# Cross-attention pairs written out as straight code, the projection between two value tiles, three residual operations on three steps

## What is computed

```python
q = proj(layernorm(x), Wq, bq); k = proj(ctx, Wk, bk); v = proj(ctx, Wv, bv)   # 16 heads of 16
scores = where(mask, clip(q @ k.T / 4, -50, 50), -50)
ctx_out = softmax(scores) @ v
delta = clip(residual_scale, 0, 0.3) * (ctx_out @ Wo.T + bo)
x = x + layernorm(delta) * ln_gamma + ln_beta
```

## Time and profile before

| what | value |
|---|---|
| device time, median of three runs | 1797.5 us (1793.64 to 1798.63) |
| device time of the profiled execution | 1795.94 us |
| its span, first to last instruction | 1794.1 us |
| cross-attention loop, first scores to last step | 538 to 1661 us of the span |
| mean granted clock of TensorE | 0.946 of full speed |

### The profile page before, as it was taken

The page is one execution under the profiler, slowest core; times in us unless marked ns, Lnnn a source line. Parts: engine busy times, 40 slices in busy tenths (PEclk is TensorE's granted clock), DMA queues, the critical chain, the costliest instruction groups (busy, mean ns, idle before and its releaser), DMA issues. The chain is left out here.

```text
span 1794.1 us, 48379 instructions
## 1 busy us (share of the span) xinstructions
PE 1594.6 (89%) x18290; PEld 1341.1 (75%) x18290; DVE 1454.5 (81%) x2513; ACT 1117.9 (62%) x2155; POOL 734.8 (41%) x743
## 2 busy tenths in 40 slices
PE   5899999998739999999999999999999999999464
PEld 5888888886528878787887787877877878788233
DVE  3788877875467898888888988888889888898698
ACT  3566555664337776676676666766766667677463
POOL 1565555553163443443343434433434344343133
PEclk9999999998769999999999999999999999999678
DMA  6000000000221111111111111111111111110001
GB/s 183 1 1 2 2 1 1 1 0 1 85 79 47 48 48 39 45 47 48 36 47 48 47 42 42 47 48 37 47 48 48 46 38 47 48 47 2 1 11 31
DMA packets 41611, 66.85 MB, mean 37 GB/s; under 512 B 7749, under 2 KB 40194, under 8 KB 41282
## 3 DMA queue, kind: packets, MB, share of 16 engines
q1 hardware_dynamic: 41410, 63.93, 12.3%
HBM read 62.08 MB, written 1.84 MB: 36 GB/s over the span
## 5 line engine op out<-in xcount | busy, mean ns | idle before, releaser
L1146 POOL TENSOR_TENSOR xa_CW<-xa_CTX,xa_CH 128x500 fp32r<-128x500 f32 x187 | 283.1, 1514 | 676.6 <-ACT xa_CH L1337 674.3
L1365 DVE TENSOR_TENSOR xl_ACC<-xl_ACC,xl_PB 125x896 f32<-125x896 f32 x320 | 422.0, 1319 | 36.1
L1329 ACT ACTIVATE xl_PB<-banks,xl_BIB,xl_SCB 125x896 f32<-125x896 f32 x384 | 400.8, 1094 | 74.5 <-PE banks L1203 74.5
L1356 DVE TENSOR_SCALAR xl_PB<-xl_PB 125x896 f32<-125x896 f32 x384 | 269.9, 703 | 57.2 <-ACT xl_PB L1329 53.6
L1311 ACT ACTIVATE xl_V<-banks 125x256 f32<-125x256 f32 x384 | 147.5, 384 | 179.6 <-PE banks L1170 179.6
L1170 PE MATMUL banks<-xa_WVhigh,xa_CH 128*125 128x256 f32 x768 | 239.5, 312 | 0.0
L1170 PE MATMUL banks<-xa_WVlow,xa_CH 128*125 128x256 f32 x768 | 217.0, 283 | 0.0
L1170 PE MATMUL banks<-xa_WVhigh,xa_CW 128*125 128x256 f32 x768 | 216.1, 281 | 0.0
L1219 PE MATMUL banks<-xl_PB,xl_V 125*32 125x112 f32 x6144 | 199.8, 271 | 2.5 <-DVE xl_PB L1356 1.7
L1302 ACT ACTIVATE xl_KXhigh<-banks,xa_bk 128x500 fp32r<-128x500 f32 x192 | 130.3, 679 | 104.2 <-PE banks L1170 104.2
L1170 PE MATMUL banks<-xa_CH,xa_WKhigh 128*128 128x500 f32 x384 | 152.5, 397 | 33.8 <-POOL xl_ONES L1108 27.7
(11 more groups left out here) (235 smaller groups left out, 4074.5 us busy)
## 6 DMA issues: line engine op xcount, KB each, us to landing
xa_CTX<-in_ctxT SPq DMA_DIRECT2D x93, 500.0 KB, 3.6
fw_WO<-in_W_o SPq DMA_DIRECT2D x1, 2048.0 KB, 17.7
xq_WR<-in_w_gating SPq DMA_DIRECT2D x1, 2048.0 KB, 9.5
X<-in_x SPq DMA_DIRECT2D x1, 1792.0 KB, 10.1
out<-ff_R SPq DMA_DIRECT2D x16, 112.0 KB, 1.9
fw_QUT<-in_W_quT SPq DMA_DIRECT2D x1, 1536.0 KB, 12.3
xa_CTX<-in_ctxT SPq DMA_DIRECT2D x1, 1500.0 KB, 14.8
xq_WL<-in_w_linear SPq DMA_DIRECT2D x1, 1024.0 KB, 11.7
```

Source lines behind the costliest of these rows:

```text
L1146: nc.gpsimd.tensor_tensor(context_piece(CW, i), context_piece(CTX, i), context_piece(CH, i), ALU.subtract).then_inc(ctx_low, 1)
L1329: nc.scalar.activation(PB[t % PR][:, :, :], banks[0:TK, 2 * i:2 * i + KT, 0:QW], ACT.Exp, scale=SCB[j][:, t:t + 1], bias=BIB[j][:, t:t + 1 ...
L1356: nc.vector.tensor_scalar(pt, pt, E_HI, E_LO, ALU.min, ALU.max).then_inc(clipped, 1)
L1365: nc.vector.tensor_tensor(ACC[j][:, :, :], prev[:, :, :], PB[t % PR][:, :, :], ALU.add).then_inc(summed, 1)
```

## The change

It does four things, all within `cross_loop`. The loop over pairs 1 to 14 becomes fourteen written-out copies on every engine. `project` moves on TensorE from ahead of both value tiles to between the first and the second. The three operations of `add_delta` move on GpSimd from step 8 to the ends of steps 6, 8 and 9, and its last wait, on its own addition, goes. To feed them, part 3 of `NORM` moves from step 7 to 6, and `delta_rstd` on ScalarE from step 6 to 5.

```diff
-    PROJECT, NORM = 3, {4: (0, 1), 5: (2,), 7: (3,), 10: (4, 5), 11: (6,)}
+    PROJECT, NORM, ADD_DELTA = 3, {4: (0, 1), 5: (2,), 6: (3,), 10: (4, 5), 11: (6,)}, (6, 8, 9)
...
         def pairs(eng, body):
 
-            body(0, True, False)
-            with eng.Fori(1, PAIRS - 1) as g:
-                body(g, False, False)
-            body(PAIRS - 1, False, True)
+            for g in range(PAIRS):
+                body(g, g == 0, g == PAIRS - 1)
...
-                def add_delta(g):
-
-                    pool.wait_ge(dn_ready, g + 1)
-                    nc.gpsimd.tensor_tensor(DL[:, :], DL[:, :], GAM[:, :], ALU.mult).then_inc(affine, 1)
-                    pool.wait_ge(affine, g * 2 + 1)
-                    nc.gpsimd.tensor_tensor(DL[:, :], DL[:, :], BET[:, :], ALU.add).then_inc(affine, 1)
-                    pool.wait_ge(affine, g * 2 + 2)
-                    xg = X[:, bass.ds(g, 1), :]
-                    nc.gpsimd.tensor_tensor(xg, xg, DL[:, :].unsqueeze(1), ALU.add).then_inc(x_added, 1)
-                    pool.wait_ge(x_added, g + 1)
+                def add_delta(g, step):
+
+                    if step == 0:
+                        pool.wait_ge(dn_ready, g + 1)
+                        nc.gpsimd.tensor_tensor(DL[:, :], DL[:, :], GAM[:, :], ALU.mult).then_inc(affine, 1)
+                    elif step == 1:
+                        pool.wait_ge(affine, g * 2 + 1)
+                        nc.gpsimd.tensor_tensor(DL[:, :], DL[:, :], BET[:, :], ALU.add).then_inc(affine, 1)
+                    else:
+                        pool.wait_ge(affine, g * 2 + 2)
+                        xg = X[:, bass.ds(g, 1), :]
+                        nc.gpsimd.tensor_tensor(xg, xg, DL[:, :].unsqueeze(1), ALU.add).then_inc(x_added, 1)
...
-                        if s == 8 and not first:
-                            add_delta(g - 1)
+                        if s in ADD_DELTA and not first:
+                            add_delta(g - 1, ADD_DELTA.index(s))
...
-                add_delta(PAIRS - 1)
+                for step in range(len(ADD_DELTA)):
+                    add_delta(PAIRS - 1, step)
...
-                def values(n, u, early=False):
-
-                    for i in range(2):
+                def values(n, u, tiles, early=False):
+
+                    for i in tiles:
...
+                        if more(last, s, 1):
+                            values(n + 1, (u + 1) % STEPS, (0,))
                         if s == PROJECT and not first:
 
                             pe.wait_ge(k_ready, n + K_AHEAD)
                             project(g - 1)
                         if more(last, s, 1):
-                            values(n + 1, (u + 1) % STEPS)
+                            values(n + 1, (u + 1) % STEPS, (1,))
...
-                        if s == 6 and not first:
+                        if s == 5 and not first:
                             delta_rstd(g - 1)
```

More of the change, by code:

```diff
@@ L1281, in _ @@
                     if p == 1:
-                        values(0, 0, early=True)
+                        values(0, 0, (0, 1), early=True)
                 pairs(pe, pair)
```

## The result

The changed kernel takes 1722.49 us in the median of four runs (1722.20 to 1724.10), the kernel before 1796.58 us: a ratio of 0.9591 with an interval of 0.9574 to 0.9607. The profiled execution has a span of 1720.7 us, 73.4 less than before. The forecast was 1731, with a range from 1720 to 1752.

A forecast was written before the change was run, and what follows sets the result against it. TensorE was taken as the bound, the gain being the excess of five long steps per pair. 29.1 + 20.4 - 4.2 + 7.6 + 12.0 = 64.9 us off 1795.94 gave 1731 us, range 1720 to 1752.

The forecast's parts named there:

- The jump: Step 11, before each of 13 jumps back: goes from 7.67 to 5.43 us, 29.1 us won.
- the rival of streams running dry: Written-out pairs on TensorE: instruction fetch falls behind, 2.24 us a hole; with three a pair, 1825 us; chance 0.02.
- The clock: Step 0 after each of 13 jumps: without the gap TensorE's clock stays up, 7.33 to 5.76 us, 20.4 us won.
- The rival built on that rule: Step 0 of the pairs: TensorE's clock falls even without the gap, the 20.4 us stay, 1751 us; chance 0.05.
- What the gap had covered: Pair boundaries: late VectorE costs 0.35 us at each of 13, 0.31 won from pair 14 to 15; together -4.2 us.
- The projection: Step 3: goes from 7.08 to 6.55 us, the keys then waiting for VectorE's read of the projection; 7.6 us won.
- The residual operations: Steps 9 and 10: spreading GpSimd's three operations removes their excess of 0.86 us in 14 pairs, 12.0 us won.
- The rival in which VectorE becomes the second bound: Steps 0, 3, 9 and 10: VectorE stays as late as before, blocking by GpSimd only moves; 1749 us, chance 0.22.

The follow-up runs named there:

- 6: Changed kernel with the engine loop back on TensorE alone, the other engines written out; span 1744.7 us in one profiled execution.
- 7: Changed kernel with the engine loop back on every engine but TensorE; span 1729.0 us in one profiled execution.
- 9: Changed kernel with a loop of two pairs per round, so 6 jumps instead of 13; span 1750.4 us in one profiled execution.
- 1: Kernel before with its loop over pairs written out, nothing else changed; 1731.15 us, ratio 0.9662.
- 4: Changed kernel with the three residual operations back in step 8, the norm's part 3 in step 7 and `delta_rstd` in step 6; 1733.42 us, ratio 0.9667.
- 8: Kernel before with VectorE's loop alone written out, the other engines still looping; 1772.72 us, span 1770.9, in one profiled execution.
- 2: Changed kernel with the engine loop over pairs back on all engines; 1760.53 us, ratio 0.9828.
- 3: Changed kernel with the projection ahead of both value tiles again; 1725.41 us, ratio 0.9618.
- 10: Changed kernel with VectorE's read of the projection ahead of the addition of tile 0 in step 3; 1721.02 us, ratio 0.9599.

## Why the prediction was right, and where it was not

**The jump** (29.1 forecast, 29.3 measured): right, and shown. TensorE's own jump makes the gap (6), the other four lie inside it (7), it goes by the number of jumps (9). In straight code TensorE had no hole in any pair, so the rival of streams running dry fell. VectorE's straight code had at least one, of 0.35 us, in step 7 of pair 14 of experiments 1, 4 and 8.

**The clock** (20.4 and 20.3): the size was right, its rule not. I took "gap, then low clock" as one thing. With the gaps in place the clock fell behind 13, 8, 4 and 1 of 13 jumps in four kernels and behind 3 of 6 in a fifth. The gap's length alone does not decide: step 11 was 7.33 long ahead of one fall in experiment 2, and 7.96 with no fall behind it in experiment 9. Without a jump no pair of any kernel saw a fall. So removing the gap is sufficient, as forecast, but 20 us was the price of this one loop, which met the fall at every jump; why it did, and the others not, stays open. The page of the Trainium skill (TensorE: Matmul & The Clock Gate, section "Why this matters for your kernels") speaks of longer idle gaps than these; the clock fell after gaps of 2 us, so here the measurement decides. The rival built on that rule fell.

**What the gap had covered** (-4.2 forecast, +0.7 measured): this is the step that failed, and it makes 4.9 of the 5.3 us by which the pairs came out better than the sum. I read the price from the boundary of pair 14 to 15, where VectorE came out of its loop code and was late for that reason: with VectorE alone written out that step took 5.83 instead of 6.42 (8). The cover was real but smaller, 0.23 (7) to 0.27 us (1), and the residual change removed those 0.27 (3).

**The projection** (7.6 and 7.9): step 3 came out at 6.53 where 6.55 was worked out, bound by VectorE's read as the text said; experiments 3 and 10 show it from both sides. Of the 0.55 in a middle pair, 0.34 is the straight code and 0.21 the move, so 3.2 of the 7.9 us belong to the projection whose name the term bears.

**The residual operations** (12.0 and 12.0): the right sum, but not by the way that was forecast, and partly by luck. Two causes overlap. With the loop kept, the residual change, beside the moved projection, took all of the 0.86 (2); without it, straight code took 0.66 (1). What both change is the order in step 7, ahead of step 8, where I had looked. GpSimd's piece starts 5.10 us into step 7 in every kernel. VectorE's second addition starts 5.20 in before, 5.04 with straight code alone, 4.92 with the loop kept, where part 3 of the norm no longer stands ahead of it, and 4.74 in the changed kernel. Behind the piece it takes 2.12 us, ahead of it 1.09. Apart from the kernel before, it came behind only in pair 14 of experiments 1, 4 and 8, and only these pairs had step 9 at 5.90 or more. This is the likely way; no run forced the order by itself, and it is not all: in experiment 8 the addition is 0.01 us ahead and steps 9 and 10 keep 0.48 of excess. With straight code in place, the residual change is worth 67.11 - 66.67 = 0.44 a pair (1 and 3), some 6 us, of which 0.27 is at the boundary. It matters more once the projection has moved, 67.18 - 66.46 = 0.72.

The rival in which VectorE becomes the second bound did not hold in the changed kernel, but it is what experiments 1 and 4 show in small. One reading in it was wrong: the blocked clip did not end with GpSimd's piece at 947.55, but at 948.04 (946.34 + 1.70), 0.49 behind it. What it said of the blocking, that it only moves, came true (1.74 at another clip), but at no price to TensorE.

Against the medians the forecast was 8.5 us high: 4.9 from the boundary, 0.4 from the rest of the sum, and the other 3.2 outside the pairs. The sum's own middle pair is 66.8, not the 66.9 stated; 66.46 was measured.

## What to carry to other kernels

Read a loop's price from its ends: an iteration that is entered from, or left into, straight code shows what the jump costs and what it covers. But a price read from loop code need not hold in straight code, where waits are on constants and end some 0.1 us sooner (VectorE's addition follows its clip after 0.04 us instead of 0.13); where two engines share a port that is enough to change who goes first. Here it took 0.66 of the 0.86 us for which the reordering had been made, and the reordering alone would have taken all of it: two cures of one fault must not be added up. And where a second engine is 90% busy, judge two edits together: the moved projection was worth 3 us with the residual change and nothing without it.

## What the runs showed of the hardware that I had not expected

- A jump back costs TensorE 1.6 to 2.5 us, and no more for a body of twice the length.
- The clock's fall after such a gap is not fixed: 13, 8, 4 and 1 of 13, and 3 of 6, for mean gaps of 2.25, 2.02, 2.04, 1.92 and 2.23 us. What decides it stays open.
- TensorE's code, written out, came in fewer packets than in the loop, 134 against 156 on its queue; the other instruction queue moved more, 70 against 45.
- An addition of VectorE that starts 0.29 us behind GpSimd's operation takes 2.04 us instead of 1.09; started 0.06 us ahead of it, it costs GpSimd the time instead (2.17 against 1.38).
